# Statistics moved from a dispatch stage into the stage before it, row stores issued ahead of weights, a rotation generator and attention norms moved between engines

## What is computed

```python
x = x + attn(layernorm(x))                       # softmax_attention, a_
x = x + retention(layernorm(x), ctx)             # retention, r_
x = x + moe_swiglu(layernorm(x))                 # moe_swiglu, mr_ and mt_
x = x + lie(layernorm(x))                        # lie_rotation, l_
x = x + one_key(layernorm(x), ctx)               # one_key_attention, q_
x = x + moe_silu(layernorm(x))                   # moe_silu, sr_ and s_

def _layernorm(x): return (x - mean(x)) / sqrt(var(x) + 1e-5)

# moe_swiglu: two of eight experts for each token
logits = einsum('bsd,de->bse', x, Wg); top_vals, top_idx = top_k(logits, 2)

# lie: per sample a 64x64 generator from the mean of its tokens
h_mean = mean(x, axis=1)
omega[:, TRIU_R, TRIU_C] = h_mean @ omega_proj_w.T + omega_proj_b
omega = omega - swapaxes(omega, -1, -2)
G = I + omega + 0.5 * omega @ omega + 1/6 * omega @ omega @ omega
lie_out = (x[:, :, :64] @ G) @ omega_out_w.T + omega_out_b
vq_out = codebook[argmax(normalize(vq_input) @ normalize(codebook).T)]
out = x + omega_mix * lie_out + vq_mix * (vq_out @ vq_proj_out_w.T + b)
return out * rsqrt(mean(out * out) + 1e-6) * norm_w

# one_key: 16 heads of width 16, one shared key and value head
qp = (q @ Wq + bq).reshape(B, H, S, hd)
out = softmax(qp @ (k @ Wk + bk).T / 16) @ (v @ Wv + bv)
```

## Time and profile before

| | |
|---|---|
| median of 3 runs | 1529.22 us (1528.43 to 1530.22) |
| the profiled execution | 1524.42 us, span 1522.0 us |
| granted TensorE clock, mean | 0.884 |
| busy shares | PE 80%, VectorE 67%, ScalarE 48%, GpSimd 27% |
| softmax attention | 0 to 185 us |
| retention | 185 to 448, one steady group 28.3 us |
| dispatch, then the experts | 448 to 540, then to 880 |
| rotation | 880 to 1041 |
| one-key attention | 1041 to 1282, one steady group 23.7 us |
| second mixture of experts | 1282 to 1522 |

### The profile page before, as it was taken

The page is one execution under the profiler, slowest core; times in us unless marked ns, Lnnn a source line. Parts: engine busy times, 40 slices in busy tenths (PEclk is TensorE's granted clock), DMA queues, the critical chain, the costliest instruction groups (busy, mean ns, idle before and its releaser), DMA issues. The chain is left out here.

```text
span 1522.0 us, 29958 instructions
## 1 busy us (share of the span) xinstructions
PE 1220.0 (80%) x10737; PEld 883.0 (58%) x10737; DVE 1013.8 (67%) x2051; ACT 728.4 (48%) x1402; POOL 416.6 (27%) x403
## 2 busy tenths in 40 slices
PE   4989589898744369999999915883799976999997
PEld 2666456776633359999999803732455542565664
DVE  5999667776654845666666566676788786567553
ACT  4778445554325224444444314034255556756743
POOL 2222255644222035455454311052011111000000
PEclk9999799999985579999999955556899997999999
DMA  7666276666309023232322172001544312133131
GB/s 276 242 238 239 95 146 113 127 108 92 57 30 402 14 70 95 91 95 91 105 95 75 49 268 96 2 1 51 148 80 92 69 25 76 51 127 119 36 126 28
DMA packets 100120, 165.08 MB, mean 108 GB/s; under 512 B 14918, under 2 KB 63882, under 8 KB 98700
## 3 DMA queue, kind: packets, MB, share of 16 engines
q1 hardware_dynamic: 90956, 138.27, 32.5%
q0 software_dynamic: 8640, 24.65, 5.1%
q10 hardware_dynamic: 384, 0.26, 0.1%
HBM read 110.67 MB, written 52.30 MB: 107 GB/s over the span
## 5 line engine op out<-in xcount | busy, mean ns | idle before, releaser
L1545 DVE TENSOR_TENSOR r_sim<-r_pS,r_causal 128x512 f32<-128x512 f32 x128 | 86.2, 681 | 56.0 <-PE r_pS L1455 55.9
L1087 POOL DMA_INDIRECT expert_results<-mt_yout,m_deliver x78 | 77.4, 992 | 150.1 <-ACT mt_yout L1175 138.1
L1120 PE MATMUL mt_pU<-mt_xh,m_w 128*128 128x256 f16 x624 | 116.2, 274 | 1.5 <-DVE mt_xl L1205 1.5
L2971 ACT ACTIVATE q_ex<-q_pE 128x512 f32<-128x512 f32 x128 | 75.7, 600 | 83.3 <-PE q_pE L2590 83.2
L1120 PE MATMUL mt_pV<-mt_xh,m_w 128*128 128x256 f16 x624 | 115.1, 273 | 0.0
L2686 DVE TENSOR_REDUCE q_mx<-q_pS 128x4 f32<-128x512 f32 x128 | 87.1, 685 | 32.1 <-PE q_pS L2569 31.7
L1131 PE MATMUL mt_pY<-m_w,mt_hh 128*128 x624 | 106.4, 273 | 1.0 <-DVE mt_hl L1219 1.0
L3253 PE MATMUL s_pY<-s_w,s_hh 128*128 128x256 f16 x576 | 99.9, 273 | 8.0 <-DVE s_hl L3473 6.6
L1169 ACT ACTIVATE mt_hh<-ahead 128x512 f16<-128x512 f32 x78 | 49.2, 630 | 118.3 <-DVE ahead L1214 118.3
L1079 POOL DMA_INDIRECT mt_xin<-token_rows,m_fetch x78 | 86.2, 1105 | 68.2 <-POOLq L778 44.7
L1211 DVE TENSOR_TENSOR ahead<-mt_pU,ahead 128x512 f32<-128x512 f32 x78 | 53.9, 691 | 58.2 <-ACT ahead L1163 58.2
(11 more groups left out here) (593 smaller groups left out, 3443.6 us busy)
## 6 DMA issues: line engine op xcount, KB each, us to landing
s_spread_share<-shares SPq DMA_DIRECT2D x32, 512.0 KB, 6.0
a_pf<-in_L_ffn_W SPq DMA_DIRECT2D x24, 512.0 KB, 6.6
m_w<-split_w SPq DMA_DIRECT2D x6, 2048.0 KB, 23.2
split_w<-a_ph SPq DMA_DIRECT2D x24, 256.0 KB, 3.8
split_w<-a_pl SPq DMA_DIRECT2D x24, 256.0 KB, 4.2
r_kstack<-k_bounce SPq DMA_DIRECT2D x48, 128.0 KB, 4.0
r_qstack<-q_bounce SPq DMA_DIRECT2D x48, 128.0 KB, 5.3
q_Q<-m_bounce SPq DMA_DIRECT2D x24, 256.0 KB, 7.7
```

Of the source, the lines that this page charges most:

```text
L1087: pool.indirect_dma_start(results[:, :], bass.IndirectOffsetOnAxis(ap=deliver[:, at:at + 1], axis=0), yout[n % 2][:, a, :], None).then_inc ...
L1120: last = pe.matmul(ps[half][:, j, :], W[x][:, e, dc, cols], (xh, xl)[y][p][:, dc, :], start=(m == 0), stop=(m == len(steps) - 1))
L1545: dve.tensor_tensor(sim[n % SIMS][:, :].rearrange("p (h t) -> p h t", t=S), pS[n % 2][:, :].rearrange("p (h t) -> p h t", t=S), repeat(tab ...
L2971: act.activation(ex[n % RING][:, :], pE[n % 2][:, :], ACT.Exp, scale=ATT).then_inc(s["exp"], 1)
```

## The change

There are four parts.

1. Retention takes, after each group's `add_out`, the statistics of the new X (`after`, offsets 35 to 37) into tiles that `decoder` holds; the dispatch has no statistics of its own.
2. In the dispatch `ACT_ROWS` = 2 of the four rows are normalised on ScalarE and two on VectorE (`norm`), and the row stores are on SyncE's queue, before the weights.
3. In the rotation the generator is four pieces by (n, h), the identity addition is on GpSimd, the copies of the squares are on ScalarE, and the squares of the loop are written to a scratch that nothing reads.
4. In one-key attention the norms and the key copy `KM` are on GpSimd; the rows are turned with a plain transpose, and the permutation is in the access pattern with which the result is read from PSUM; statistics, turning and reading of a group are due two or more units earlier, `unturn` and what follows one unit later.

The dispatch:

```diff
+            for g in range(NG):
+                sp.wait_ge(s["xn"], ACT_ROWS * (g + 1))
+                sp.wait_ge(s["xn_dve"], (GB - ACT_ROWS) * (g + 1))
+                sp.dma_start(A["token_rows"][:, :].rearrange("(p b) d -> p b d", b=B)[:, g * GB:(g + 1) * GB, :],
+                             rows[g % ROWS_RING][:, :, :]).then_inc(rows_out[g % ROWS_RING], 16)
             for source, w in weights:
                 sp.dma_start(w, source).then_inc(weights_in, 16)
...
-                for b in range(g * GB, g * GB + GB):
+                for b in range(g * GB, g * GB + ACT_ROWS):
...
-            store(0)
             invert(2)
-            store(1)
             invert(3)
-            for g in range(2, NG):
...
+            def norm(g):
+                if g >= ROWS_RING:
+                    dve.wait_ge(rows_out[g % ROWS_RING], 16 * (g // ROWS_RING))
+                    dve.wait_ge(s["turned"], g - ROWS_RING + 1)
+                for b in range(g * GB + ACT_ROWS, g * GB + GB):
+                    dve.tensor_scalar(rows[g % ROWS_RING][:, b % GB, :], X[:, b, :], mean[:, b:b + 1], rstd[:, b:b + 1],
+                                      ALU.subtract, ALU.mult).then_inc(s["xn_dve"], 1)
+
...
             negate(0)
+            norm(0)
             dve.wait_ge(s["gate_high"], 1)
             dve.scalar_tensor_tensor(flat(Wg[1][:]), gate_w, SCALE, flat(Wg[0][:]), ALU.mult, ALU.subtract)\
                .then_inc(s["gate_low"], 1)
...
+                if g % 2 == 0 and g + 2 < NG:
+                    negate(g // 2 + 1)
                 take_low(g)
+                if g + 2 < NG:
+                    norm(g + 2)
 
```

Retention:

```diff
+                    for b, at in enumerate((35, 35, 36, 36)):
+                        g = due(t, at)
+                        if g is not None:
+                            if b == 0:
+                                dve.wait_ge(s["x_done"], g + 1)
+                            after.rows(dve, X, g, b)
+                    g = due(t, 37)
+                    if g is not None:
+                        after.combine(dve, g)
```

The rotation:

```diff
-                omega(24, 32)
+                omega(24, 32).then_inc(s["omega"], 1)
...
-                        pe.wait_ge(s["shift16"], 2)
+                        pe.wait_ge(s["shift_taken"], 1)
                     power(h, om, om, "squared")
...
-                        act.wait_ge(s["x"], g - 1)
                     for b in range(GB):
-                        act.activation(z[:, g % 2, b, :], y[:, g % 2, b, :], ACT.Square, accum_out=ss[:, g % 2, b:b + 1])\
+                        act.activation(unread[:, g % 2, b, :], y[:, g % 2, b, :], ACT.Square, accum_out=ss[:, g % 2, b:b + 1])\
                            .then_inc(s["sqd"], 1)
...
+                keep_square(0)
+                keep_square(1)
...
+                    at = each(h * HALF, HALF)
+                    pool.wait_ge(s["om"], h + 1)
+                    pool.tensor_tensor(omI[:, at, :], om[:, at, :], repeat(ident[0:LD, 0:LD], HALF), ALU.add)\
+                        .then_inc(s["omI"], 1)
                 pool.wait_ge(s["eps"], 1)
...
-                    mark(dve.tensor_tensor(om[:, at, :], om0[:, at, :], repeat(sign[:, :], HALF), ALU.mult), "om", h + 1)
...
+                def generator(n, h):
+                    at, columns = each(h * HALF, HALF), each(n * LD // 2, LD // 2)
+                    step(dve.scalar_tensor_tensor(
+                        om0[:, at, columns].rearrange("p b j -> p j b"),
+                        p1[n][0:LD, :].rearrange("p (j b) -> p j b", b=B)[:, :, at], 1.0 / PSCALE / HSCALE,
+                        spread(bp[:, columns], HALF), ALU.mult, ALU.add))
+                    return dve.tensor_tensor(om[:, at, columns], om0[:, at, columns], repeat(sign[:, columns], HALF), ALU.mult)
 
                 def half_way(h):
                     at = each(h * HALF, HALF)
+                    dve.wait_ge(s["m2"], h + 1)
+                    dve.wait_ge(s["omI"], h + 1)
                     step(dve.scalar_tensor_tensor(G[:, at, :], m2[:, at, :], -0.5, omI[:, at, :], ALU.mult, ALU.add))
...
+                dve.wait_ge(s["omega"], 1)
+                step(generator(0, 0))
                 dve.wait_ge(s["hot_turned"], 1)
                 mark(dve.tensor_copy(v["hotT"][:, :], pV[0:CODES, 224:224 + B]), "hotT")
+                step(generator(0, 1))
                 dve.wait_ge(s["code_taken"], 1)
                 step(dve.tensor_tensor(v["dif"][:, :], pV[0:B, 256:256 + LD], v["vq"][:, :], ALU.subtract))
...
-                generator(0)
+                dve.wait_ge(s["woo_high"], 1)
+                dve.tensor_tensor(Woo16[1][:, :], Woo_mixed[0:LD, :], Woo16[0][0:LD, :], ALU.subtract).then_inc(s["woo_low"], 1)
+                dve.wait_ge(s["omega"], 2)
+                mark(generator(1, 0), "om", 1)
                 dve.wait_ge(s["vq_out"], 1)
-                step(dve.tensor_tensor(v["sh1"][:, :], pShift, bvo[:, :], ALU.add))
+                mark(dve.tensor_tensor(v["sh1"][:, :], pShift, bvo[:, :], ALU.add), "shift_taken")
+                mark(generator(1, 1), "om", 2)
...
                                               ALU.subtract), "shift16", 2)
-                generator(1)
-                with_identity(0)
-                with_identity(1)
-                dve.wait_ge(s["woo_high"], 1)
-                dve.tensor_tensor(Woo16[1][:, :], Woo_mixed[0:LD, :], Woo16[0][0:LD, :], ALU.subtract).then_inc(s["woo_low"], 1)
-                keep_square(0)
                 half_way(0)
-                keep_square(1)
+                finish_G(0)
                 half_way(1)
-                finish_G(0)
                 G_low(0)
                 finish_G(1)
                 G_low(1)
```

One-key attention:

```diff
-    WEIGH_AT, TURN_AT, FINISH_AT, ADD_AT = 2, 4, 5, 6
+    WEIGH_AT, TURN_AT, FINISH_AT, ADD_AT = 2, 5, 6, 7
...
 
+        def natural(dc):
+            return pP[:, dc, :].rearrange("p (b c r) -> p b r c", c=HD, r=HEAD_ROWS)
+
+        def tokens(t):
+            return t.rearrange("p (b r c) -> p b r c", c=HD, r=HEAD_ROWS)
...
                     for b in range(GB):
-                        last = pe.matmul(pP[:, dc, keys(b)], xn[:, b, dc * P:(dc + 1) * P], natural[:, :], start=True,
-                                         stop=True)
+                        last = pe.transpose(pP[:, dc, keys(b)], xn[:, b, dc * P:(dc + 1) * P], ident[:, :])
                     last.then_inc(s["turned"], 1)
...
-                        g = due(i, u, -39 + a)
+                        g = due(i, u, -41 + a)
...
-                    dve.tensor_tensor(xl[:, dc, :], pP[:, dc, :], xh[:, dc, :], ALU.subtract).then_inc(s["xl"], 1)
+                    dve.tensor_tensor(tokens(xl[:, dc, :]), natural(dc), tokens(xh[:, dc, :]), ALU.subtract)\
+                       .then_inc(s["xl"], 1)
...
-                    for b, at in enumerate((-55, -54, -53, -50)):
+                    for b, at in enumerate((-57, -56, -55, -52)):
...
-                    for b, at in enumerate((-45, -45, -42, -41)):
-                        g = due(i, u, at)
-                        if g is not None:
-                            norm(g, b)
...
-                    act.activation(xh[:, dc, :], pP[:, dc, :], ACT.Copy).then_inc(s["xh"], 1)
+                    act.activation(tokens(xh[:, dc, :]), natural(dc), ACT.Copy).then_inc(s["xh"], 1)
...
+                def norm(g, b):
+                    if b == 0:
+                        pool.wait_ge(s["rstd"], g + 1)
+                        pool.wait_ge(s["turned"], DC * g)
+                    pool.tensor_scalar(xn[:, b, :], X[:, g * GB + b, :], rs.mean[:, b:b + 1], rstd[:, b:b + 1],
+                                       ALU.subtract, ALU.mult).then_inc(xn_done, 1)
+
+                def copy_keys(g):
+                    pool.wait_ge(s["kl"], g + 1)
+                    if g == 0:
+                        pool.wait_ge(s["made"], 2)
+                    if g >= 2:
+                        pool.wait_ge(s["scored"], turns["unit", g - 2, UNITS - 1] + 1)
```

131 lines of the change are left out of this document (46 added, 85 removed).

## The result

The changed kernel takes **1482.96 us** (median of 4 runs, 1480.29 to 1483.89) against 1528.89 us of the kernel before; the ratio is 0.9695 (95% interval 0.9679 to 0.9712). Measured again later beside the kernel before, it was 1486.86 against 1525.85, ratio 0.9739 (0.9721 to 0.9758). Medians of one kernel thus differ by 3 to 4 us from one session to the next, and the gain is 39 to 46 us. The forecast was 1497, range 1484 to 1510: the direction and the three places were right, the size too small by a fifth to a third.

The account below looks back on a forecast made before the run. It took the row-buffer wait beside the weights (dispatch), VectorE's line and a shared scratch (rotation), and PE (one-key) as limits: -16.5 - 6.5 - 9 = -32 from 1524.42 gives 1492.4, plus 4.8 is 1497.2; range 1484 to 1510, 80%.

Parts of the forecast that it names:

- -16.5: Dispatch and retention costed together: eight groups and the last split end at 483.3 against 499.97.
- -6.5: Rotation: generator -3.5 and loop -3 together, bounds -4.5 and -7.6.
- -9: One-key attention: shorter TensorE waits and lighter VectorE, less stepped reads and lead-in; bounds 0 and -13.
- 2.3 us hide: Retention, groups 0 to 3: each group's added statistics and small operations fit VectorE's idle gaps at no cost.
- 2.85 us a group: Dispatch: TensorE as limit, eight transposes of 1.97 us plus about 0.9 for the logit matmuls.
- Rival (c): Dispatch: PE's clock rises; at 2.4 GHz a group costs 2.1 us, -5, total 1492; chance 12%.
- rival (a): Dispatch: the row ring still holds, 4 us a group, 8 to 9 us less gain, total 1506; chance 15%.
- the dispatch 75 us: Dispatch: its length, named as one sign that the forecast is right.
- -3.5: Rotation before the loop: generator partly earlier, sums and copies moved off VectorE; cubes end at 980.4 instead of 983.8.
- -3: Rotation loop: own scratch for squares; pace from 5.51 to 4.75 to 5.3 us over five groups, plus 0.5.
- The 9.2 should go nearly whole: One-key attention: PE's 9.2 us wait in 155 us for ScalarE's results vanishes with output transposes at five units.
- half of 5.2: One-key attention: lighter VectorE removes about half of PE's 5.2 us wait for maxima before the scores.

Follow-up runs that it names:

- the experiment: Changed kernel with only group 6's retention statistics moved behind the last group's reciprocal, and group 0's one-key norms on VectorE: 1476.33 us, ratio 0.9672 to the kernel before.

## Why the prediction was wrong, step by step

The limits and waits that the forecast named in the dispatch and the rotation were the right ones. What failed is the size of three terms of its sum, -16.5 (measured -20.1), -6.5 (-9.5) and -9 (-12.1 and -10.7), and the 4.8 us added to the sum at its end.

**The sum against one execution.** The step "the median of the runs shown is 4.8 above that execution, so the prediction is 1497.2" cost 5.4 of the 14 us: the offset belonged to the execution drawn, not to the program. The changed kernel's profiled execution is 0.6 above its median in the first session and 1.2 below in the second. The second session's 1486.86 lies within the forecast's range. The trace's own sum, -32 against -40.8, is what was wrong of the reasoning.

**Retention**: right. +4.3 was forecast to the last X, +3.6 measured, by two errors that partly cancel: groups 4 and 5 cost 0.7 where 2 was charged, and group 6's statistics ahead of the last variance sum were 2.3 by the forecast, 2.9 in the trace, 3.1 by the experiment. That the statistics hide in groups 0 to 3 was right for the place where the change put them, and the forecast's reason ("2.3 us hide" since "VectorE idles") was too weak: the same operations a few units later do not hide.

**Dispatch**: the chain and its order were right, the first transposes came at 459.54 (458.2 forecast). Mis-sized was "2.85 us a group": 2.42 measured, so 3.4 us in eight groups. I had added durations of operations that overlap. The row of eight transposes, 1.97 us, holds the last one's latency, and the logits begin inside it: they start at 466.31 while the transposes run from 464.57 for 1.94. Start-to-start distances are the measure. Rival (c) came true in part and gave little: PEclk is 0.50 up to 470 and 0.78 from 470 to 482, where one group of eight transposes takes 1.07 us, but the groups still start 2.4 us apart (472.01, 474.45, 476.81), since TensorE waits 0.69 us for VectorE's low part behind the short one. Weights stayed hidden, rival (a) did not happen. The sign "the dispatch 75 us" does not follow from the forecast's own split: 93.9 - 20.8 from the last X, less the 4.7 that fall into retention (the addition, the statistics, the crossing), is about 68, and 65.9 was measured.

**Rotation**: mis-sized twice, and past its bounds (-4.5 and -7.6). "-3.5" for the generator was -4.0; no run undoes that part alone, and since the old code ahead of the loop took 107.1 us in one trace and 108.6 in another, it is known to 1.5 us only. "-3" for the loop was -5.5: the forecast counted five groups at the slow pace where the additions to X kept it for six distances, and I gave VectorE's slowed `finish` a pace of its own (4.75 to 5.3), while per group VectorE has 2.7 + 1.2 + 0.7 = 4.6 us, just TensorE's 4.64. The rows for that sum were there. Nor do the two engines slow "each other": GpSimd's addition takes 2.34 us alone (the last one, 1037.61 in the kernel before) and 2.35 beside `finish`. The port rule of the Trainium skill, "SBUF — State Buffer", section "Who interferes with whom", agrees with the shared 2.69 us (1.66 alone) and with one shift operation that took 2.67 us at 950.12 while GpSimd's identity sum ran; its 5 us for the rotation in place of 6.5 did not come, since neither stood on the path.

**One-key attention**: -9 was forecast, -12.1 and -10.7 measured, inside its bounds of 0 and -13; over the six traces of the same code it is -9.4 to -12.1, so the number was near. But the reasons were half right. "The 9.2 should go nearly whole" holds only together with the norms' move, which I priced at half of 5.2 (that wait shrank by 1.7). "As many 128x128 matmuls as before" was wrong: the matmul with `natural` was two instructions for a block, the transpose is one, which the trace of before could have told by its count; it is worth some 2 us. "I take 0.7" for GpSimd's norm was 1.22, and still hidden: four norms and four additions take 7.8 us of the 10.4. The stepped reads cost nothing (672 and 597 ns against 676 and 605), against my +0.35. The cachelines note of that page of the Trainium skill, "Door 1: The DMA port swizzle", speaks of matmuls; carried over to reads by VectorE and ScalarE, as the forecast did with its -6, it does not hold here.

**The range.** All terms leaned to the small side. Its low end rests on a full one-key gain and the warmer clock (1488), and has no place for a rotation past its bounds or for a faster group in the dispatch at the low clock.

## What to carry to other kernels

- Two waits of one engine can hide each other: an edit that removes one may show nothing, or a loss (2.2 us here), until the other engine is relieved too. Try such edits in pairs before dropping one.
- Take an engine's need per round from start to start of equal rows, and never from the sum of the rows' durations; and add up each engine's row separately before giving one of them a pace.
- Work hides in a place, not in an engine's idle share. Put small operations right where the engine waits, look what the other engines run beside them there, and ask of the last round what they delay.
